# Epsilon as a third triple of the variance aggregation, in a one-layer vision tower

## The reference

```
h   = patches @ W.T + b
a   = layer_norm(h + conv_block(h), gamma, beta)      # conv_block: 16 heads, softmax over 31 taps
h1  = (h + a - mean) / sqrt(var + 1e-5)
f   = bitlinear(silu(bitlinear(h1, w_gate)) * bitlinear(h1, w_up), w_down)
out = (h1 + f - mean) / sqrt(var + 1e-5)
layer_norm(x) = (x - mean) * rsqrt(var + 1e-5) * gamma + beta
```

## Time and profile before

| | us |
|---|---|
| runs | 126.51, 127.45, 126.32 (median 126.51) |
| span of the profiled execution | 125.7 |
| PE busy | 107.9 (86%) |
| DVE busy | 86.1 (69%) |
| POOL busy | 80.8 (64%) |
| ACT busy | 66.1 (53%) |

### The profile page before, as it was taken

How to read it: one execution, slowest core, us unless ns; L and a number is a source line. 1 busy time by engine, 2 the same in 40 slices (tenths; PEclk the granted TensorE clock), 3 DMA queues, 4 the chain that set the end, 5 groups by cost and what they waited for, 6 DMA issues and landing times.

```text
span 125.7 us, 2379 instructions
## 1 busy us (share of the span) xinstructions
PE 107.9 (86%) x718; PEld 67.8 (54%) x718; DVE 86.1 (69%) x202; ACT 66.1 (53%) x109; POOL 80.8 (64%) x153
## 2 busy tenths in 40 slices
PE   6997999999999999999999999999998653884400
PEld 2673465866856486467555576668573322453200
DVE  5014593644965768799998999888696676898410
ACT  0042128639527444594633988766783836575200
POOL 6994000059700865867974868798888888888870
PEclk9999999999999999999999999999999999689975
DMA  3899999962321122232313112212300100011112
GB/s 104 260 357 340 399 420 422 400 255 21 63 24 17 42 25 23 53 51 42 32 42 30 14 42 25 22 42 27 64 0 0 42 0 0 4 46 42 44 43 82
DMA packets 23467, 12.45 MB, mean 99 GB/s; under 512 B 18141, under 2 KB 21981, under 8 KB 23070
## 3 DMA queue, kind: packets, MB, share of 16 engines
q1 hardware_dynamic: 21936, 10.46, 29.4%
q10 hardware_dynamic: 1518, 1.84, 4.8%
HBM read 9.95 MB, written 2.34 MB: 98 GB/s over the span
## 4 chain that ended last, share of the span: by engine, by line
PE 63%; POOL 19%; issue 5%; DMA 4%; ACTq 2%; DVE 2%; POOLq 1%
PE bank L339 12%; PE bank L417 11%; PE bank L400 11%; PE bank L383 6%; PE bank L444 5%; POOL q L1080 5%; DMA bias_cols<-in_cols 4%; PE bank L472 4%; PE bank L488 3%; POOL rstd L999 3%; POOL f L1087 3%; PE bank L357 3%; ACTq L676 2%; POOL res L1055 2%; POOL veps L998 2%
## 5 line engine op out<-in xcount | busy, mean ns | idle before, releaser
L339 PE MATMUL bank<-xT,tokW 128*128 128x256 f32 x72 | 16.7, 381 | 0.0
L417 PE MATMUL bank<-conv_w,vpad 128*32 128x128 f32 x256 | 15.8, 398 | 0.0
L1043 POOL TENSOR_TENSOR taps<-probs,inv_total 128x256 f32<-128x256 f32 x8 | 5.1, 634 | 15.7 <-DVE inv_total L741 15.4
L339 PEld LDWEIGHTS bank<-xT,tokW 128*128 128x128 f32 x72 | 13.5, 190 | 2.6 <-issue 0.9
L400 PE MATMUL bank<-wl,h1T 128*128 128x496 f32 x32 | 14.6, 578 | 0.0
L641 ACT ACTIVATE gu<-bank,sc 128x512 f32<-128x512 f32 x16 | 11.0, 686 | 5.3 <-PE bank L472 5.1
L527 PE MATMUL bank<-w_q,q2T 128*128 128x256 f16 x64 | 8.5, 273 | 3.9 <-ACT q2T L655 3.5
L812 DVE TENSOR_TENSOR gu<-gu,bank 128x512 f32<-128x512 f32 x16 | 10.8, 681 | 1.3 <-ACT gu L641 0.6
L998 POOL TENSOR_SCALAR veps<-mv 128x1 f32<-128x1 f32 x16 | 3.6, 225 | 11.9 <-DVE mv L751 10.9
L417 PEld LDWEIGHTS bank<-conv_w,vpad 128*32 128x32 f32 x256 | 8.3, 122 | 5.2 <-issue 1.4
L1080 POOL TENSOR_SCALAR q<-gu,sc 128x512 f16<-128x512 f32 x14 | 10.0, 716 | 1.4 <-DVE sc L829 0.2
(11 more groups left out here) (119 smaller groups left out, 237.2 us busy)
## 6 DMA issues: line engine op xcount, KB each, us to landing
xT<-in_xT SPq DMA_DIRECT2D x3, 768.0 KB, 16.9
w_raw<-in_wg SPq DMA_DIRECT2D x1, 1024.0 KB, 13.2
w_raw<-in_wu SPq DMA_DIRECT2D x1, 1024.0 KB, 15.2
w_raw<-in_wd SPq DMA_DIRECT2D x1, 1024.0 KB, 16.9
shear<-taps SPq DMA_DIRECT2D x8, 128.0 KB, 1.8
conv_w<-shear SPq DMA_DIRECT2D x64, 16.0 KB, 2.0
out_dram<-res SPq DMA_DIRECT2D x8, 128.0 KB
tokW<-in_tokW SPq DMA_DIRECT2D x6, 128.0 KB, 5.0
```

The costliest lines, as they stand in the source:

```text
L339: last = nc.tensor.matmul(ps_embed(pair, m), tokW[:, k, m * P:(m + 1) * P], xT[:, pair, k, :], start=(k == 0), stop=(k == KC_PATCH - 1))
L417: last = nc.tensor.matmul(ps_yT[j * SLOT:(j + 1) * SLOT, k, :], vpad[:, s, h, :], conv_w[:, s, :, h], start=(par == 0), stop=(par == 1))
```

## The change

`stats` gets nine columns instead of six. Columns 6 to 8 of each of its six slots are written once, early, by two memsets on DVE: count 0, mean 0, and 256 times epsilon as the count times variance. bn_stats goes on writing columns 0 to 5. bn_aggr reads all nine and so gives the variance with epsilon in it. The additions of epsilon on POOL and their link go, and the pow reads `mv` directly. The first attn_variance waits for the memsets; inv_std_mid gets two waits, for the h3 and the limit of two tiles earlier, which read the `rstd` buffer that its pow overwrites.

```diff
--- before.py
+++ after.py
@@ -106,9 +106,8 @@
         taps = sb("taps", [P, 2, IMAGES, HEADS])
         conv_w = sb("conv_w", [P, SLOTS, P, HEADS])
         yT = sb("yT", [P, 2, KC, P])
-        stats = sb("stats", [P, 3, 2, 6])
+        stats = sb("stats", [P, 3, 2, 9])
         mv = sb("mv", [P, 3, 2, 2])
-        veps = sb("veps", [P, 3, 2, 1])
         rstd = sb("rstd", [P, 3, 2, 2])
         shift_out = sb("shift_out", [P, 2])
         a1 = sb("a1", [P, D])
@@ -223,6 +222,7 @@
         wscale_ok = sem("wscale_ok")
         mean_read = sem("mean_read")
         dve_step = sem("dve_step")
+        eps_ok = sem("eps_ok")
 
         ones_ok = sem("ones_ok")
         const_ok = sem("const_ok")
@@ -743,10 +743,12 @@
             def attn_stats(t):
 
                 dve.wait_ge(attn_ps, t + 1)
-                at["attn", t] = mark(nc.vector.bn_stats(stats[:, 0, t % 2, :], ps_attn))
+                at["attn", t] = mark(nc.vector.bn_stats(stats[:, 0, t % 2, 0:6], ps_attn))
 
             def attn_variance(t):
 
+                if t == 0:
+                    dve.wait_ge(eps_ok, 1)
                 after(at["attn", t])
                 nc.vector.bn_aggr(mv[:, 0, t % 2, :], stats[:, 0, t % 2, :]).then_inc(var_attn, 1)
 
@@ -771,7 +773,7 @@
             def mid_stats(t):
 
                 dve.wait_ge(h1b_read, t + 1)
-                at["mid", t] = mark(nc.vector.bn_stats(stats[:, 1, t % 2, :], a2[:, t % 2, :]))
+                at["mid", t] = mark(nc.vector.bn_stats(stats[:, 1, t % 2, 0:6], a2[:, t % 2, :]))
 
             def mid_variance(t):
 
@@ -886,7 +888,7 @@
                     dve.wait_ge(f_ok, t + 1)
                 else:
                     after(at["f", t])
-                at["out", t] = mark(nc.vector.bn_stats(stats[:, 2, t % 2, :], f[:, t % 3, :]))
+                at["out", t] = mark(nc.vector.bn_stats(stats[:, 2, t % 2, 0:6], f[:, t % 3, :]))
 
             def out_variance(t):
 
@@ -946,6 +948,8 @@
                 bias_rows(0, LOGITS)
 
             nc.vector.memset(vpad[:], 0.0).then_inc(zeros_ok, 1)
+            nc.vector.memset(stats[:, :, :, 6:8], 0.0)
+            nc.vector.memset(stats[:, :, :, 8:9], D * LN_EPS).then_inc(eps_ok, 1)
             dve.wait_ge(cols_in, 16)
             nc.vector.tensor_copy(b1_rep[:], b1.unsqueeze(2).broadcast_to([P, KC, P])).then_inc(b1_rep_ok, 1)
             dve.wait_ge(const_ok, 1)
@@ -995,8 +999,7 @@
 
             def inv_std(j, t, done):
 
-                link(nc.gpsimd.tensor_scalar(veps[:, j, t % 2, :], mv[:, j, t % 2, 1:2], LN_EPS, 1.0, ALU.add, ALU.mult))
-                nc.gpsimd.tensor_tensor(rstd[:, j, t % 2, 0:1], veps[:, j, t % 2, :], minus_half[:],
+                nc.gpsimd.tensor_tensor(rstd[:, j, t % 2, 0:1], mv[:, j, t % 2, 1:2], minus_half[:],
                                         ALU.pow).then_inc(done, 1)
 
             def inv_std_attn(t):
@@ -1011,8 +1014,9 @@
                 pool.wait_ge(var_mid, t + 1)
                 if t >= 2:
                     pool.wait_ge(scale_ok, t - 1)
-                link(nc.gpsimd.tensor_scalar(veps[:, 1, t % 2, :], mv[:, 1, t % 2, 1:2], LN_EPS, 1.0, ALU.add, ALU.mult))
-                link(nc.gpsimd.tensor_tensor(rstd[:, 1, t % 2, :], veps[:, 1, t % 2, :].broadcast_to([P, 2]), halves[:],
+                    pool.wait_ge(h3_ok, t - 1)
+                    pool.wait_ge(inner_min_ok, t - 1)
+                link(nc.gpsimd.tensor_tensor(rstd[:, 1, t % 2, :], mv[:, 1, t % 2, 1:2].broadcast_to([P, 2]), halves[:],
                                              ALU.pow))
                 if t >= 4:
                     pool.wait_ge(q1_scale_ok, t - 3)
```

## The result

The changed kernel takes 121.66 us in the median of 4 runs (121.3 to 121.97), the kernel before 126.53 (4 runs, 126.32 to 127.45). The ratio is 0.9597, 95% interval 0.9559 to 0.9635: 4.0% faster, 4.87 us. The forecast was 122.3 us in 121.3 to 124.2.

A forecast was written before the change was run, and what follows sets the result against it. PE was taken to bound the kernel up to 76.6 us, POOL's list from there to 121.64. Gain 4.48 - 0.12 - 0.1 = 4.26 us; 125.7 - 4.26 + 0.81 gave 122.3 us, range 121.3 to 124.2.

The forecast's parts named there:

- The two regimes: PE is full from 11.0 to 76.6 us; afterwards POOL runs through its list, so only removals there shorten the kernel.
- 0.28 us an addition, 4.48 in all: Sixteen late additions on POOL, each 0.28 us from veps start to pow start, give 4.48 us; the early eight nothing.
- No gain from stalls and gaps: Two long additions (0.48, 0.44 us) beside DVE: their extra 0.29 and 0.25 counted as no gain, the pow inheriting the stalls.
- 0.12 lost at add_beta(6): At 86.86 us, its ACT copy lets POOL move up 1.00 us where four removed additions ask 1.12.
- 0.1 lost at the store: Last result on DVE waits for the store of result(5): landing about 2.3 us, distance 2.33 after; 0.1 us lost.
- over 0.6 spare on the last tile: Last tile's statistics ready at 119.15, its pow at 120.24 on the same scale: over 0.6 us left, POOL stays last.
- The conversion: From profiled span to run time: the median 126.51 lies 0.81 us above the span of 125.7, so 0.81 is added.
- (a): Rival: PE caps the shift, down(3) moving only 1.6 us; 3.3 us remain, 123.2 us; chance 18%.
- (b): Rival: only the tail gains, the five last additions, 1.4 us, giving 125.1 us; chance 7%.
- (c): Rival: the pow takes over the cost, growing from 0.55 to 0.83 us, nothing won, 126.5 us; chance 5%.
- (d): Rival: PE's clock falls to 1.2 GHz for all of 96.9 to 118.2 us, giving 128.3 us; chance 4%.
- The signs: Expected after: pows unchanged, POOL without input waits 77 to 118, tail results 1.66 us apart, less PE idle, bn_aggr near 0.20.

The follow-up runs named there:

- experiment 2: Changed kernel with only the eight early additions (tiles 0 to 3, attention and middle) back, adding 0: 121.42 us against 121.66.
- experiment 3: Changed kernel with only the sixteen late additions (attention and middle tiles 4 to 7, all output tiles) back, adding 0: 124.91 us.
- experiment 1: Changed kernel with all 24 additions back on POOL, each linked to its pow, adding 0 (table column "24 of 0"): 124.99 us.
- 24 of 0, no link: Changed kernel with all 24 additions of 0 back, but without link, the pow reading the variance itself: 123.38 us.
- experiment 6: Three kernels: changed with 24 linked additions of 1e-5 and third triple zero, 126.78 us; before adding 0, 125.00; before with stats nine wide, 126.81.
- experiment 5: Changed kernel with only the last five additions (output tiles 3 to 7) back, adding 0: 122.31 us.
- experiment 7: Changed kernel with three result buffers instead of two: 121.17 us.
- experiment 8: Changed kernel with eight extra matmuls keeping PE busy near the end: 121.64 us; the same with three result buffers: 120.96 us.

## Why the prediction was right, point by point

**The two regimes.** Right. The early eight additions are free (experiment 2), the late sixteen carry the cost (experiment 3 against 1).

**0.28 us an addition, 4.48 in all.** Right for the addition and its link, too low for what a removal gives back: the price left out the gap ahead of the addition, and so it was 0.40 in ten of sixteen places. To see it whole, POOL's time from start to start, summed over the length of the table by the kind of instruction:

| us behind | before | 24 of 0 | 24 of 0, no link | after |
|---|---|---|---|---|
| addition (15) | 4.66 | 4.32 | 2.34 | |
| pow | 10.15 | 9.94 | 10.22 | 9.89 |
| small scales (sc) | 3.26 | 3.13 | 2.89 | 2.87 |
| add_h3 | 5.13 | 4.76 | 4.79 | 4.70 |
| h3 | 3.04 | 2.64 | 2.67 | 2.60 |
| add_beta | 2.47 | 2.22 | 2.22 | 2.20 |
| quantisation | 8.89 | 8.93 | 9.08 | 9.52 |
| result, shift, taps | 7.12 | 6.92 | 6.84 | 7.28 |
| sum | 44.72 | 42.86 | 41.05 | 39.06 |

The additions' own steps go, 4.66. The steps of other instructions shrink by 1.79, and 0.79 comes back as new waits behind a quantisation and a result: 5.66 us in all. The first of the sixteen lies ahead of this length.

**No gain from stalls and gaps.** Too cautious, and the largest term that the sum lacks. Ten additions had a gap of 0.09 ahead of them where the pow, or an addition of 0, starts at -0.03: 10 x 0.12 = 1.2 us, shown by experiment 6. The stalls beside DVE were not all inherited. Two that the prediction didn't name, on POOL before:

```profile
77.47 0.58 POOL L1029 TENSOR_SCALAR sc<-sc,rstd,inner_min 128x1 f32<-128x1 f32 x1
...
85.23 0.77 POOL L1064 TENSOR_SCALAR h<-centred,rstd 128x256 f32<-128x256 f32 x1
```

Elsewhere these take 0.34 and 0.48. With the quantisation at 91.45 (0.98) and the two additions (0.48 and 0.44) that is 1.36 us of stall before; after, one quantisation lasts 0.94 (77.58) and one pow 0.68 (90.61), 0.38 in all. So 1.0 us of stalls went, 0.54 of it the additions' own. I had expected the pow to inherit them. One does (90.61), but whether two instructions of POOL and DVE meet changes with every shift of the lists.

**0.12 lost at add_beta(6).** The right instruction, mis-sized: POOL waits 0.64 us there. The limit was as worked out, but POOL came some 0.3 us earlier than the four additions ask, and the ACT copy 0.2 us later than before:

```profile
85.62 0.37 ACT L609 COPY h1b<-bank 128x256 f32<-128x256 f32 x1
```

The wait is no accident of this execution: the profiles of experiments 5, 7 and 8 have it with 0.63 or 0.64 us too. Why the copy comes later against the start of POOL's full stretch isn't shown.

**0.1 lost at the store, over 0.6 spare on the last tile.** Both too small. The store takes 2.60 us to its semaphore, not the 2.3 that I read from the traffic, and the last result can start 2.72 us behind result(5), where the forecast left it 2.33: 0.4 us are lost. Experiment 7 takes this wait away. The reserve of the last tile was used up, by POOL's larger gain and by PE's clock at the lower level: 0.24 us of waiting in the profiled execution.

**Nine elements at 18 ns, memsets at nothing.** Measured 14 ns, 68 ns and 63 ns; hidden.

**The conversion.** I set the profiled span of 125.7 against the median and got 0.81 us around it. It is some 1.8, and that execution was 1.0 us longer than the median. Since the forecast is in the end the median less the sum, the error cancels, by luck and not by reasoning.

**Rivals.** (a) and (b), a cap by PE or only the tail: POOL waits for ACT and DVE at four places behind 76.6 (0.18, 0.23, 0.64 and 0.24), but the shift goes on behind them. (c), the pow takes the cost: no, 556 ns. (d), the clock: before it was granted at 0.50 to 0.76 from 107 to 111, after it stays at 1.00 there and falls near 111.5; that costs the last pow 0.24 us and the kernel nothing while the last result waits for its store (experiment 8).

**The signs.** As forecast: the pows, an aggregation near 0.20, and less idle time of PE between 96.9 and 103.7 (0.59, 0.61 and 0.31 us instead of 0.99, 0.80 and 1.06). Not as forecast: POOL waits for an input four times between 77 and 118, and from result to result in the tail are 1.53 us (113.33 to 114.86), not 1.66, where before there were 1.94 (118.79 to 120.73):

```profile
120.73 0.55 POOL L1055 TENSOR_SCALAR res<-f,rstd,shift_out 128x256 f32<-128x256 f32 x1
```

So an addition was worth 0.41 there, 0.28 and its gap. And two of the three things that were to show the prediction wrong happened: POOL was idle behind ACT between 84 and 111, 0.64 us at add_beta(6), and the last result waited 0.4 us for a store. These mechanisms were named and priced at 0.2 us together; they took 1.0 and were outweighed.

Net: 4.26 was forecast, 4.87 measured. What was left out (1.2 of gaps, 1.0 of stalls) outweighs what was taken too small (0.5 at add_beta, 0.3 at the store, 0.2 at the last tile). These terms give 5.4 us, and in the two profiled executions the way from the addition or pow of attention tile 4 to the last result did shrink by 5.6 (122.23 - 76.64 against 116.60 - 76.59); the medians differ by less, 4.87, as the profiled execution of before was a long one. So the number is near because errors of opposite sign nearly met. The range held because its low end had the stalls in it, not because the gap was seen.

## What to carry to other kernels

Find the stretch in which an engine has no idle time for want of an input, and price a removed instruction there with its link and with the gap ahead of it: here 0.28 us from start to start for 0.19 of work, of which half was the wait of an engine for its own last instruction, and 0.12 more where the next instruction starts without the gap. Work that folds a constant into data that another engine with time to spare reads anyway cost 14 ns of that engine here. When the bound engine moves by several microseconds, look for the next limits at the end of the kernel: here a wait for the reuse of a buffer, and behind it one for a slow last tile that gained nothing when it alone was taken away.

## What the runs showed of the hardware that was not expected

- A GpSimd tensor_scalar that adds 1e-5 starts 0.08 to 0.10 us after the end of its predecessor; the same instruction adding 0 starts some 0.03 us ahead of that end, in 10 of 16 places. With the stalls that went with it, that is worth 1.6 us of this kernel (126.65 to 125.00). Only these two values were tried; what property of the immediate decides is open.
- On GpSimd, subtract then multiply with two pointer operands takes 1247 ns for 128 x 256, multiply then add 549.
- A store of 128 KB is complete 2.60 us after the result that it reads, 0.3 to 0.5 us after its traffic has ceased (in the changed kernel 70 GB/s from 116.00 to 116.25 us, nothing from 116.25 to 116.50, the semaphore at 116.51).
- bn_aggr over nine elements instead of six takes 14 ns more (195 for 181). The kernel is written so that the third triple (count 0, mean 0, 256 times epsilon) puts epsilon into the variance; no row shows the value that comes out.
